# GNN kernel on one core: 64 source rows of every group are brought by SyncE's direct DMAs, and POOL's gathers of five chunks become shorter

## The chip, the core and the metric

One core of a Trainium2 chip. The number is the device time of one execution in microseconds (us), the median of several runs; lower is better.

## What is computed

Three layers of a relational graph network over 6250 nodes with 256 features, 200,000 edges sorted by destination, 8 edge types, and then a feed-forward layer on each node:

```python
for l in range(3):
    xr = jnp.einsum('nd,rde->rne', x, W_rel[l])
    msg = xr[edge_type, src]
    agg = jax.ops.segment_sum(msg, dst, num_segments=x.shape[0])
    x = jax.nn.relu(agg + x @ W_root[l] + bias[l])
# around it: x = x0 + gnn(layernorm(x0)); x = x + ffn(layernorm(x)), ffn in the log domain
```

The step that matters here is `msg[..., src]`: for every edge the 1 KB row of its source node is read from a table in HBM, 200,000 rows a layer.

## The kernel before, in words

The edges are cut into **chunks** of 128 (one edge a partition), three chunks make a **triple**, and nine triples (27 chunks, 3456 edges) a **group**. A layer has 58 groups, the last of which has 8 triples. Three layers make 174 groups.

The tile `rows` is a ring of 27 chunk slots, one group deep: slot (k, j) holds chunk j of triple k, 128 partitions by 256 floats.

- **POOL** (L393 to L403) fills the ring. For each chunk it issues one indirect DMA: 128 indices of `idx`, one row of the node table for each. Before triple k of a group it waits on `seg_ready` until TensorE has finished triple k of the group before, since it overwrites that slot. Each gather counts `gathered[k]` up by 16.
- **PE** waits for the three gathers of a triple (`rows_of`, L425), multiplies the rows by a one-hot matrix of (type, destination) (L421, 12 instructions a triple), and raises `seg_ready`. Once a group it multiplies the sums by the 8 relation matrices (L492).
- **DVE** adds the sums into `agg` (L1003), makes the one-hot matrices of the next group (L908) and adds a group's result to the node sums (L1025, L1026).
- **ACT** zeroes `agg`, and ends and stores finished tiles of 128 nodes.
- **SP** (SyncE) has little to do in layer 0: one 128 KB load of a node tile a group (`load_tile`, L329). In layers 1 and 2 it fetches the last chunk (8, 2) of every odd group but the last, row by row: it reads 32 source numbers into registers (L347), issues 32 one-row DMAs into the buffer `far_rows` (L352), and so four times. DVE copies `far_rows` into the ring slot at the head of the odd group (`take_fetched`, L969 to L975) and thereby frees the buffer for SP's next fetch. POOL leaves out that gather (the `CH - 1` of L398).

The order of POOL's gathers is the plain order of groups, triples and chunks. In the set-up SP issues the loads of the weights, of the source numbers for its own fetches (`far_idx`, L308) and of small tables, from which DVE makes the groups' places before the first product can start.

```python
for j in range(CH - 1 if layer and g % 2 and k == TPG - 1 else CH):
```

Of the kernel before, what the change touches and what calls it, by code (L numbers as in the profile page):

```python
# [7 lines left out]
P = 128  # L8
# [4 lines left out]
CH = 3  # L13
# [20 lines left out]
FETCHED = GROUPS // 2 - 1  # L34
HALF = P // 2
LOADS = 32
LN_EPS = 1e-5
LOG_EPS = 1e-8
assert TRIPLES == FULL_TRIPLES + 2 and 0 < TAIL < TE and BLOCKS == FULL_BLOCKS + 1 and TILES == XC * XCHUNKS + 1
assert WIN * R == P and GROUPS > TILES and GROUPS == 2 * FETCHED + 2  # L40


def gnn_ffn(nc, x, src, dst, etype, w_rel, w_root, gnn_bias, ffn_w, ffn_b, out):
    fp32, bf16 = mybir.dt.float32, mybir.dt.bfloat16
    i32, u32 = mybir.dt.int32, mybir.dt.uint32
# [7 lines left out]
    tables = [nc.dram_tensor(f"node_table{i}", [NP_, D], fp32, kind="Internal").ap() for i in range(2)]  # L53
    span_dram = nc.dram_tensor("triple_span", [2, BLOCKS * P], fp32, kind="Internal").ap()
# [5 lines left out]
    with ctx:  # L60
# [20 lines left out]

        far_idx = at("far_idx", [1, FETCHED * P], i32, edges_at)
        assert FETCHED * P * 4 <= 2 * edge_bytes
# [16 lines left out]
        far_rows = sb("far_rows", [P, D], fp32)  # L100
# [120 lines left out]
        far_idx_loaded = sem("far_idx_loaded")  # L221
        far_fetched = [[sem(f"far_fetched{l}_{h}") for h in range(2)] for l in range(1, L)]
        far_copied = sem("far_copied")
# [52 lines left out]
        def _(sp):  # L276
# [22 lines left out]
            for c, (lo, hi) in enumerate(x_chunks):  # L299
# [33 lines left out]
            with sp.Fori(0, TILES) as g:  # L333
                load_tile(g, g)
            with sp.Fori(TILES, GROUPS) as g:
                load_tile(g, TILES - 1)
            for layer in range(L - 1):
                sp.wait_ge(out_ready, (layer + 1) * GROUPS)
                sp.wait_ge(stored, 16 * TILES * (layer + 1) + 16)
                load_weights(layer + 1)  # L340
                sp.wait_ge(far_idx_loaded, 16)
                with sp.Fori(0, FETCHED) as i:

                    sp.wait_ge(far_copied, i * 2 + (layer * 2 * FETCHED + 2))
                    sp.sem_inc(sp_mark, 1)
                    for q in range(P // LOADS):
                        _, nodes = nc.values_load_multi_w_load_instructions(  # L347
                            far_idx[0:1, ds(i * P + q * LOADS, LOADS)], engines=[SP], min_val=0, max_val=N - 1,
                            skip_runtime_bounds_check_because="sources are nodes")
# [8 lines left out]
        def _(pool):  # L358
# [31 lines left out]
            for layer in range(L):  # L390
# [740 lines left out]
```

## Time and profile before

| what | us |
| --- | --- |
| median of 3 runs | 5964.4 |
| the runs | 5960.87 to 5973.35 |
| span of the profiled execution | 5964.9 |
| its own time beside the span | not given apart |
| POOL busy | 4396.5 (74%) |
| PE busy | 4310.7 (72%) |
| DVE busy | 1844.7 (31%) |
| ACT busy | 619.0 (10%) |

POOL's busy time is the time in which its cores work on a gather; what its sequencer needs between two gathers is not counted as busy, so 74% need not mean that POOL had time to spare. Issuing a DMA on SP is not counted as busy either and is read from the view of the line that issues it.

### The profile page before, as it was taken

What the parts mean: (1) busy time and instruction counts of PE and PEld (TensorE: products, weight loads), DVE (VectorE), ACT (ScalarE), POOL (GpSimd) and SP (SyncE); (2) the same over time, 40 slices, a digit from 0 to 9 for tenths busy, and PEclk for the clock granted to TensorE, in tenths of its full rate; (3) what the DMA queues carried; (4) which work ended last, traced back from release to release, by engine and by line L of the source; (5) the groups of instructions that cost most, each with busy time, mean ns of one, the idle gap of its engine ahead of it and who ended that gap; (6) DMA issues with size and microseconds to landing.
All of it is one profiled execution on the core that took longest, in us unless ns stands there. A gap on an engine that the chain in (4) does not pass through costs nothing.

```text
span 5964.9 us, 107654 instructions
## 1 busy us (share of the span) xinstructions
PE 4310.7 (72%) x26040; PEld 3901.4 (65%) x26041; DVE 1844.7 (31%) x3589; ACT 619.0 (10%) x848; POOL 4396.5 (74%) x4659
## 2 busy tenths in 40 slices
PE   4777777777777767777777777766776777776776
PEld 3666666666676656666666666666676666666666
DVE  5222222222222222222222222223333334333333
ACT  3001010010101000000000001000101011101111
POOL 5777777777777677777777777767777777777774
PEclk8898989898989888889999999888888888888887
DMA  6333333333333333333333333333333333333332
GB/s 196 113 111 113 112 112 112 111 114 111 113 112 112 107 111 110 111 111 111 110 111 111 111 110 112 110 106 113 114 113 115 113 113 114 114 113 114 113 113 74
DMA packets 296167, 674.77 MB, mean 113 GB/s; under 512 B 86202, under 2 KB 147387, under 8 KB 295772
## 3 DMA queue, kind: packets, MB, share of 16 engines
q0 software_dynamic: 222384, 607.55, 35.2%
q1 hardware_dynamic: 44686, 37.38, 2.1%
q10 hardware_dynamic: 28702, 26.46, 1.3%
q14 instruction: 378, 3.10, 0.2%
q8 instruction: 17, 0.28, 0.0%
HBM read 645.38 MB, written 25.68 MB: 112 GB/s over the span
## 4 chain that ended last, share of the span: by engine, by line
PE 27%; POOL 25%; issue 20%; SPq 15%; DMA 6%; DVEq 3%; DVE 3%; ACT 1%; ACTq 0%
POOL rows L403 25%; PE bank L421 15%; SPq L352 13%; PE bank L492 10%; DMA rows<-node_table,idx 5%; SPq L347 3%; DVE agg L1003 1%; ACT agg L708 1%; DVEq L986 1%; DVEq L989 1%; PE bank L618 1%; DVEq L1093 1%; PE bank L611 0%; DVE onehot L908 0%; PE bank L537 0%
## 5 line engine op out<-in xcount | busy, mean ns | idle before, releaser
L403 POOL DMA_INDIRECT rows<-node_table,idx x4633 | 4389.2, 947 | 1504.1 <-issue 1316.2
L421 PE MATMUL bank<-onehot,rows 128*128 128x128 f32 x18792 | 2700.1, 305 | 1422.5 <-DVE agg L1003 705.8
L421 PEld LDWEIGHTS bank<-onehot,rows 128*128 128x128 f32 x18792 | 2564.0, 218 | 1571.8 <-issue 1553.2
L1003 DVE TENSOR_TENSOR agg<-bank,agg 128x256 f32 x1566 | 663.7, 424 | 2079.8 <-PE bank L421 1575.6
L492 PE MATMUL bank<-wrel,agg 128*128 128x256 f32 x5568 | 1273.8, 388 | 44.4 <-DVE agg L1016 34.2
L492 PEld LDWEIGHTS bank<-wrel,agg 128*128 128x128 f32 x5568 | 1073.4, 195 | 200.0 <-issue 53.9
L908 DVE TENSOR_TENSOR onehot<-bank,key 128x1152 f32<-128x1152 f32 x525 | 707.0, 1347 | 0.0
L708 ACT COPY agg<-zero_col 128x2304 f32 x174 | 367.2, 2111 | 2928.9 <-PE bank L492 2928.9
L1025 DVE SCALAR_TENSOR_TENSOR acc<-bank,in_first,acc 128x256 f32 x174 | 84.2, 484 | 1777.6 <-PE bank L492 1680.9
L611 PE MATMUL bank<-wroot,nextT 128*128 128x256 f32 x392 | 146.7, 510 | 0.0
L715 ACT COPY acc<-bank 128x256 f32 (+1 forms) x98 | 36.5, 372 | 1004.7 <-PE bank L611 1004.7
L611 PEld LDWEIGHTS bank<-wroot,nextT 128*128 128x128 f32 x392 | 85.3, 241 | 55.2 <-issue 45.3
L599 PE MATMUL bank<-ident_bf,sgn 128*128 128x128 bf16 x98 | 16.2, 258 | 121.5 <-issue 115.1
L599 PEld LDWEIGHTS bank<-ident_bf,sgn 128*128 128x128 bf16 x98 | 6.5, 100 | 130.0 <-issue 130.0
L609 PE MATMUL bank<-bias_bc,one_row 1*128 1x256 f32 x196 | 90.3, 549 | 1.3 <-ACT nextT L723 1.3
L723 ACT COPY nextT<-bank 128x256 f32<-128x256 f32 x98 | 36.5, 372 | 462.2 <-PE bank L592 462.2
L1026 DVE SCALAR_TENSOR_TENSOR acc<-bank,in_second,acc 128x256 f32 x174 | 82.6, 475 | 0.0
L537 PE MATMUL bank<-wroot,xT 128*128 128x256 f32 x232 | 78.7, 474 | 0.0
L1016 DVE TENSOR_TENSOR agg<-agg 128x256 f32<-128x256 f32 (+1 forms) x174 | 72.7, 418 | 0.0
L537 PEld LDWEIGHTS bank<-wroot,xT 128*128 128x128 f32 x232 | 56.7, 248 | 11.0
L975 DVE COPY rows<-far_rows 128x256 f32<-128x256 f32 x56 | 19.1, 340 | 144.8 <-DMA far_rows<-node_table 113.6
L618 PE MATMUL bank<-wT,magT 128*128 128x256 f32 x196 | 51.4, 386 | 0.9 <-ACT sgnT L741 0.9
(138 smaller groups left out, 800.1 us busy)
## 6 DMA issues: line engine op xcount, KB each, us to landing
far_rows<-node_table SPq DMA_DIRECT2D x7168, 1.0 KB
rows<-node_table,idx POOLq DMA_INDIRECT x4633
node_table<-new_x ACTq DMA_DIRECT2D x98, 128.0 KB
x_tile<-node_table SPq DMA_DIRECT2D x58, 128.0 KB, 2.2
x_in<-in_x_dram SPq DMA_DIRECT2D x8, 768.0 KB, 11.2
wrel<-in_L_gnn_W_rel_dram SPq DMA_DIRECT2D x6, 1024.0 KB, 8.2
xres<-in_x_dram ACTq DMA_DIRECT2D x48, 128.0 KB
out_dram<-res ACTq DMA_DIRECT2D x48, 128.0 KB
```

The lines of the kernel that those rows point to most:

```text
L347: _, nodes = nc.values_load_multi_w_load_instructions(far_idx[0:1, ds(i * P + q * LOADS, LOADS)], engines=[SP], min_val=0, max_val=N - 1, ...
L352: sp.dma_start(far_rows[p:p + 1, :].rearrange("o (a b) -> o a b", a=2), tables[(layer + 1) % 2][ds(nodes[m], 1), :].rearrange("o (a b) -> ...
L403: pool.indirect_dma_start(rows[:, s:s + D], None, tables[layer % 2], bass.IndirectOffsetOnAxis(ap=idx[:, g * TPG + k, j:j + 1], axis=0),). ...
L421: last = nc.tensor.matmul(to[:, h, :], of[:, s:s + P], hot[:, hot_k * CH + j, :], start=(j == 0), stop=(j == CH - 1))
L492: last = nc.tensor.matmul(out_ps, agg[:, half * KH + h, r, 0:P], wrel[:, h, r * D:(r + 1) * D], start=(r == 0 and h == 0), stop=(r == R - ...
L537: last = nc.tensor.matmul(root_ps, xT[:, h, :], wroot[:, 0, h, :], start=(h == 0), stop=(h == KH - 1))
L609: nc.tensor.matmul(next_ps, one_row[:, :], bias_bc[0:1, layer + 1, :], start=True, stop=False)
L611: last = nc.tensor.matmul(next_ps, nextT[:, h, :], wroot[:, layer + 1, h, :], start=False, stop=(h == KH - 1))
L618: nc.tensor.matmul(lns_ps, magT[:, h, :], wT[:, h, :], start=(h == 0), stop=(h == KH - 1))
L708: nc.scalar.copy(agg[:, ds(g % 2 * KH, KH), :, :].rearrange("p h r s -> p (h r s)"), zero_col[:, :].to_broadcast([P, KH * R * SLOTS])).the ...
L908: return nc.vector.tensor_tensor(onehot[:, b, :, :], place_ps.unsqueeze(1).to_broadcast([P, BATCH * CH, P]), key[:, ds(g * TPG + b * BATCH ...
L1003: nc.vector.tensor_tensor(window, seg[k % 3].rearrange("p h (r w) -> p h r w", r=R), window, ALU.add).then_inc(agg_added, 1)
```

## The change

In all 57 full groups of all three layers, POOL's gathers of five chunks get shorter: chunks (7,1) and (7,2) by their last 4 rows, (8,0) by 8, (8,1) by 16, (8,2) by 32, 64 rows in all. SP brings these 64 rows by one-row DMAs straight into the ring slots. For that it waits, as POOL does, until triples 7 and 8 of the group before have been multiplied. The whole-chunk fetch, the buffer `far_rows`, DVE's copy and the left-out gather go away. SP's table of sources is now five strided loads from `src`, and DVE shifts it once so that it holds byte offsets; PE waits for SP's landings as well as for the gathers. The diff, cut to its core:

```diff
-FETCHED = GROUPS // 2 - 1
-HALF = P // 2
+FETCHED = GROUPS - 1
+TAILS = ((TPG - 2, 1, 4), (TPG - 2, CH - 1, 4), (TPG - 1, 0, 8), (TPG - 1, 1, 16), (TPG - 1, CH - 1, 32))
...
+    table_bytes = [t.rearrange("n d -> (n d)").bitcast(u8).unsqueeze(0) for t in tables]
...
             sp.wait_ge(turned, 11)
+            full_groups = src[0:FETCHED * TPG * TE].rearrange("(o g e) -> o g e", o=1, e=TPG * TE)
+            m = 0
+            for i, (k, j, n) in enumerate(TAILS):
+                end = (k * CH + j + 1) * P
+                q, m = (1, 0) if i == len(TAILS) - 1 else (0, m)
+                sp.dma_start(far_at[q:q + 1, :, m:m + n], full_groups[:, :, end - n:end]).then_inc(far_at_loaded, 16)
+                m += n
             load_weights(0)
-            full_groups = src[0:(GROUPS - 2) * TPG * TE].rearrange("(g e) -> g e", e=TPG * TE)
-            sp.dma_start(far_idx[:, :].rearrange("o (g e) -> o g e", e=P),
-                         full_groups[1::2, TPG * TE - P:TPG * TE].unsqueeze(0)).then_inc(far_idx_loaded, 16)
...
-            for layer in range(L - 1):
-                sp.wait_ge(out_ready, (layer + 1) * GROUPS)
-                sp.wait_ge(stored, 16 * TILES * (layer + 1) + 16)
-                load_weights(layer + 1)
-                sp.wait_ge(far_idx_loaded, 16)
-                with sp.Fori(0, FETCHED) as i:
-                    sp.wait_ge(far_copied, i * 2 + (layer * 2 * FETCHED + 2))
...
-                    for q in range(P // LOADS):
...
-                        for m in range(LOADS):
-                            p = q * LOADS + m
-                            sp.dma_start(far_rows[p:p + 1, :].rearrange("o (a b) -> o a b", a=2),
-                                         tables[(layer + 1) % 2][ds(nodes[m], 1), :].rearrange("o (a b) -> o a b", a=2)
-                                         ).then_inc(far_fetched[layer][p // HALF], 16)
+            def fetch(layer, g):
+                def tail(i, starts, landed):
+                    k, j, n = TAILS[i]
+                    s = (k * CH + j) * D
+                    for p, start in zip(range(P - n, P), starts):
+                        sp.dma_start(rows[p:p + 1, s:s + D].bitcast(u8), table_bytes[layer % 2][:, ds(start, ROW_BYTES)]).then_inc(landed, 16)
+
+                few = starts_of(g, 0, LOADS)
+                if layer or not isinstance(g, int):
+                    sp.wait_ge(seg_ready, g * TPG + (layer * TRIPLES - 1))
+                    sp.sem_inc(sp_mark, 1)
+                tail(0, few[0:4], far_in_eighth[layer])
+                tail(1, few[4:8], far_in_eighth[layer])
+                if layer or not isinstance(g, int):
+                    sp.wait_ge(seg_ready, g * TPG + layer * TRIPLES)
+                    sp.sem_inc(sp_mark, 1)
+                tail(2, few[8:16], far_in_ninth[layer][0])
+                tail(3, few[16:32], far_in_ninth[layer][0])
+                tail(4, starts_of(g, 1, LOADS), far_in_ninth[layer][1])
+
+            load_tile(0, 0)
+            sp.wait_ge(far_at_ready, 1)
+            fetch(0, 0)
+            load_tile(1, 1)
+            with sp.Fori(1, TILES - 1) as g:
+                fetch(0, g)
+                load_tile(g + 1, g + 1)
...
+            for layer in range(1, L):
+                sp.wait_ge(out_ready, layer * GROUPS)
+                load_weights(layer)
+                sp.wait_ge(stored, 16 * TILES * layer + 16)
+                with sp.Fori(0, FETCHED) as g:
+                    fetch(layer, g)
...
-                        for j in range(CH - 1 if layer and g % 2 and k == TPG - 1 else CH):
+                        for j in range(CH):
                             s = (k * CH + j) * D
+                            own = P - sum(n for *at, n in TAILS if at == [k, j] and g < FETCHED)
                             pool.indirect_dma_start(
-                                rows[:, s:s + D], None, tables[layer % 2],
-                                bass.IndirectOffsetOnAxis(ap=idx[:, g * TPG + k, j:j + 1], axis=0),
+                                rows[0:own, s:s + D], None, tables[layer % 2],
+                                bass.IndirectOffsetOnAxis(ap=idx[0:own, g * TPG + k, j:j + 1], axis=0),
                             ).then_inc(gathered[k], 16)
...
+                if k == TPG - 2:
+                    with pe.If(g < FETCHED):
+                        pe.wait_ge(far_in_eighth[layer], g * (16 * 8) + 16 * 8)
...
+                if k == TPG - 1:
+                    with pe.If(g < FETCHED):
+                        pe.wait_ge(gathered[k], g * (16 * CH) + (layer * FETCHED + 1) * (16 * CH))
+                        for h, n in ((0, 24), (1, LOADS)):
+                            pe.wait_ge(far_in_ninth[layer][h], g * (16 * n) + 16 * n)
...
+            dve.wait_ge(far_at_loaded, 16 * len(TAILS))
+            nc.vector.tensor_single_scalar(far_at[:, :, :], far_at[:, :, :], ROW_SHIFT, ALU.arith_shift_left).then_inc(far_at_ready, 1)
...
-            def take_fetched(layer, g):
...
-                nc.vector.tensor_copy(rows[:, s:s + D], far_rows[:, :]).then_inc(far_copied, 2)
```

POOL's instructions, before: the end of an odd group of layer 1 and the head of the next. Each row is one form of gather with how many follow one another; the second row is the last triple, with two gathers in place of three.

```order
L403 DMA rows<-node_table,idx 128x256 [waits seg_ready]
L403 DMA rows<-node_table,idx 128x256 x2
L403 DMA rows<-node_table,idx 128x256 [waits seg_ready]
L403 DMA rows<-node_table,idx 128x256
L403 DMA rows<-node_table,idx 128x256 [waits seg_ready]
L403 DMA rows<-node_table,idx 128x256 x2
```

POOL's instructions after the change, the last three triples of any full group and the head of the next:

```order
L432 DMA rows<-node_table,idx 128x256 [waits seg_ready]
L432 DMA rows<-node_table,idx 128x256 x2
L432 DMA rows<-node_table,idx 128x256 [waits seg_ready]
L432 DMA rows<-node_table,idx 124x256 x2
L432 DMA rows<-node_table,idx 120x256 [waits seg_ready]
L432 DMA rows<-node_table,idx 112x256
L432 DMA rows<-node_table,idx 96x256
L432 DMA rows<-node_table,idx 128x256 [waits seg_ready]
```

The number of gathers of an odd group goes from 26 to 27, and five of the 27 now cover fewer partitions.

SP's instructions, before: the head of the loop that fetches a chunk. The pair of rows at L352 stands 32 times behind each of the four loads of L347.

```order
L347 ISA [waits far_copied]
L347 TENSOR_LOAD far_idx
L352 ISA
L352 DMA far_rows<-node_table 1x256
L352 ISA
L352 DMA far_rows<-node_table 1x256
L352 ISA
```

SP's instructions after the change, one pass of the loop of layer 1 or 2 (in layer 0 a load of `x_tile` stands behind it):

```order
L341 TENSOR_LOAD far_at
L356 ISA
L352 DMA rows<-node_table 1x1024 [waits seg_ready]
L352 DMA rows<-node_table 1x1024 x7
L361 REGISTER_ALU
L352 DMA rows<-node_table 1x1024 [waits seg_ready]
L352 DMA rows<-node_table 1x1024 x23
L341 ISA
L341 TENSOR_LOAD far_at
L352 DMA rows<-node_table 1x1024 x32
```

One pass now serves one group in place of two, with 64 rows and two loads of registers; the address instruction ahead of each one-row DMA is gone, and the waits are on `seg_ready` and no longer on DVE's copy.

## Rows read from the trace of the kernel before

**Rows 1.** The page: span, busy time of each engine, and the gathers' group.

```profile
span 5964.9 us, 107654 instructions
...
PE 4310.7 (72%) x26040; PEld 3901.4 (65%) x26041; DVE 1844.7 (31%) x3589; ACT 619.0 (10%) x848; POOL 4396.5 (74%) x4659
...
L403 POOL DMA_INDIRECT rows<-node_table,idx x4633 | 4389.2, 947 | 1504.1 <-issue 1316.2
```

**Rows 2.** Timeline of POOL alone, layer 0, steady state: start, length, idle before.

```profile
1099.98 0.94 POOL L403 DMA_INDIRECT rows<-node_table,idx  x1 [0.30 <-PE bank L421]
1101.23 0.94 POOL L403 DMA_INDIRECT rows<-node_table,idx  x1 [0.30 <-issue]
1102.47 0.94 POOL L403 DMA_INDIRECT rows<-node_table,idx  x1 [0.30 <-issue]
1103.72 0.94 POOL L403 DMA_INDIRECT rows<-node_table,idx  x1 [0.30 <-issue]
```

**Rows 3.** The gathers by stretch: set-up, layers 0, 1, 2, the gaps, the end.

```profile
0.00:50.50 50.50, 0.00 (x0) 1.00 0.95 318
50.50:2011.30 1960.80, 1478.49 (x1563) 0.90 0.39 113
2011.30:2036.50 25.20, 0.00 (x0) 0.77 0.04 10
2036.50:3956.40 1919.90, 1452.18 (x1535) 0.90 0.39 112
3956.40:3982.60 26.20, 0.00 (x0) 0.70 0.03 11
3982.60:5908.90 1926.30, 1458.50 (x1535) 0.86 0.39 115
5908.90:5964.90 56.00, 0.00 (x0) 0.71 0.03 9
```

**Rows 4.** Line L403 over the whole span: shortest, median, longest gather, idle before.

```profile
L403 POOL DMA_INDIRECT rows<-node_table,idx x4633: 941/946/1201, 50.8 to 5907.8; - x194
```

**Rows 5.** Waits of POOL within 3000 to 3900 us (total, times, longest).

```profile
POOL rows L403 <- issue: 200.6, 658, 0.3
POOL rows L403 <- PE bank L421: 18.9, 62, 0.3
```

**Rows 6.** SP's lines in the window 2118.6 to 2184.8 us, one fetch of 128 rows.

```profile
L352 SPq FUSED_REGOPS  x128: 37/37/37, 2120.8 to 2183.4; - x128
L352 SPq MOVE far_rows<-node_table x128: 29/29/29, 2120.9 to 2183.5; - x128
L352 SPq DMA_DIRECT2D far_rows<-node_table x128: 224/225/282, 2120.9 to 2183.6; - x128
...
L347 SPq TENSOR_LOAD <-far_idx x5: 2028/2030/2032, 2118.7 to 2183.9; - x5
```

**Rows 7.** Timeline of SP, 32 one-row DMAs between two register loads.

```profile
2120.92 13.26 SPq L352 DMA_DIRECT2D far_rows<-node_table  x32
```

**Rows 8.** DMA queue of the gathers (packets, MB, share of 16 engines).

```profile
q0 software_dynamic: 222384, 607.55, 35.2%
```

**Rows 9.** Chain that ended last, 3000 to 3200 us: the landing of a gather.

```profile
3027.14 2.72 DMA rows<-node_table,idx
```

**Rows 10.** Timeline of SP in the set-up.

```profile
50.63 1.01 SPq L279 DMA_DIRECT2D wrel<-in_L_gnn_W_rel_dram  x2
51.68 1.60 SPq L308 DMA_DIRECT2D far_idx<-in_src_dram  x1
53.33 1.55 SPq L311 DMA_DIRECT2D wroot<-in_L_gnn_W_root_dram  x3
54.92 1.88 SPq L314 DMA_DIRECT2D span<-triple_span  x2
```

**Rows 11.** Timeline of POOL, the first gather of the second group.

```profile
90.94 0.94 POOL L403 DMA_INDIRECT rows<-node_table,idx  x1 [6.40 <-PE bank L421]
```

**Rows 12.** DVE's copy of a fetched chunk, over the whole span.

```profile
L975 DVE COPY rows<-far_rows x56: 281/294/543, 2101.1 to 5846.5; 128x256 f32<-128x256 f32 x56
```

More of the change, by code:

```diff
@@ L32 @@
 XCHUNKS = 8
[L34 to L35 removed]
+FETCHED = GROUPS - 1
+TAILS = ((TPG - 2, 1, 4), (TPG - 2, CH - 1, 4), (TPG - 1, 0, 8), (TPG - 1, 1, 16), (TPG - 1, CH - 1, 32))
 LOADS = 32
+ROW_BYTES = D * 4
+ROW_SHIFT = 10
 LN_EPS = 1e-5
@@ L39 @@
 assert TRIPLES == FULL_TRIPLES + 2 and 0 < TAIL < TE and BLOCKS == FULL_BLOCKS + 1 and TILES == XC * XCHUNKS + 1
-assert WIN * R == P and GROUPS > TILES and GROUPS == 2 * FETCHED + 2
+assert WIN * R == P and GROUPS > TILES and ROW_BYTES == 1 << ROW_SHIFT
 def gnn_ffn(nc, x, src, dst, etype, w_rel, w_root, gnn_bias, ffn_w, ffn_b, out):
     fp32, bf16 = mybir.dt.float32, mybir.dt.bfloat16
-    i32, u32 = mybir.dt.int32, mybir.dt.uint32
+    i32, u32, u8 = mybir.dt.int32, mybir.dt.uint32, mybir.dt.uint8
     ALU = mybir.AluOpType
@@ L219, in gnn_ffn @@
         w_taken = sem("w_taken")
-        far_idx_loaded = sem("far_idx_loaded")
-        far_fetched = [[sem(f"far_fetched{l}_{h}") for h in range(2)] for l in range(1, L)]
-        far_copied = sem("far_copied")
+        far_at_loaded = sem("far_at_loaded")
+        far_at_ready = sem("far_at_ready")
+        far_in_eighth = [sem(f"far_in_eighth{l}") for l in range(L)]
+        far_in_ninth = [[sem(f"far_in_ninth{l}_{h}") for h in range(2)] for l in range(L)]
         gathered = [sem(f"gathered{k}") for k in range(TPG)]
@@ new lines, in starts_of @@
+            def starts_of(g, q, n):
+                _, starts = nc.values_load_multi_w_load_instructions(
+                    far_at[q:q + 1, ds(g, 1), 0:n].rearrange("q g m -> q (g m)"), engines=[SP], min_val=0, max_val=(N - 1) * ROW_BYTES,
+                    skip_runtime_bounds_check_because="sources are nodes")
+                return starts
+            def fetch(layer, g):
[7 more added lines that the diff above has]
+                    sp.wait_ge(seg_ready, g * TPG + (layer * TRIPLES - 1))
+                    sp.sem_inc(sp_mark, 1)
+                tail(0, few[0:4], far_in_eighth[layer])
[6 more added lines that the diff above has]
+                tail(4, starts_of(g, 1, LOADS), far_in_ninth[layer][1])
@@ new lines, in _ @@
+            load_tile(0, 0)
[5 more added lines that the diff above has]
+                load_tile(g + 1, g + 1)
+            with sp.Fori(TILES - 1, FETCHED) as g:
+                fetch(0, g)
+                load_tile(g + 1, TILES - 1)
+            for layer in range(1, L):
[4 more added lines that the diff above has]
+                    fetch(layer, g)
@@ L428, in rows_of @@
                     pe.wait_ge(gathered[k], gg * (16 * CH) + 16 * CH)
-                elif layer == 0:
-                    with pe.If(g < GROUPS - 1):
-                        pe.wait_ge(gathered[k], g * (16 * CH) + 16 * CH)
+                if k == TPG - 2:
+                    with pe.If(g < FETCHED):
+                        pe.wait_ge(far_in_eighth[layer], g * (16 * 8) + 16 * 8)
                         pe.sem_inc(pe_mark, 1)
-                else:
-                    before = (GROUPS - 1) * 16 * CH + (layer - 1) * 16 * ((GROUPS - 1) * CH - FETCHED)
-                    with pe.If(g < GROUPS - 1):
-                        with pe.If(g % 2 > 0):
-                            pe.wait_ge(gathered[k], g * (16 * CH - 8) + (before + 16 * CH - 8))
-                            pe.wait_ge(far_copied, g + ((layer - 1) * 2 * FETCHED + 3))
-                            pe.sem_inc(pe_mark, 1)
-                        with pe.Else():
-                            pe.wait_ge(gathered[k], g * (16 * CH - 8) + (before + 16 * CH))
-                            pe.sem_inc(pe_mark, 1)
+                if k == TPG - 1:
[3 more added lines that the diff above has]
+                            pe.wait_ge(far_in_ninth[layer][h], g * (16 * n) + 16 * n)
                         pe.sem_inc(pe_mark, 1)
@@ L967, in extra_tiles @@
                     dve.sem_inc(dve_mark, 1)
-            def take_fetched(layer, g):
-                for h in range(2):
-                    dve.wait_ge(far_fetched[layer - 1][h], g * (8 * HALF) + 8 * HALF)
-                held(g)
-                s = (TPG * CH - 1) * D
-                nc.vector.tensor_copy(rows[:, s:s + D], far_rows[:, :]).then_inc(far_copied, 2)
             def group(layer, g, late=None):
                 gg = g + layer * GROUPS
-                if layer == 1 and g % 2 and g < GROUPS - 1:
-                    take_fetched(layer, g)
-                if layer == L - 1:
-                    with dve.If(g < GROUPS - 1):
-                        with dve.If(g % 2 > 0):
-                            take_fetched(layer, g)
-                        dve.sem_inc(dve_mark, 1)
                 _, places = nc.values_load_multi_w_load_instructions(
```

13 lines of the change are left out of this document (2 added, 11 removed).

## The prediction, made before the changed kernel was run

> **What bounds the kernel now.** I read the page first, then POOL alone in time, then the gathers by stretch, then SP. On the page no engine is busy over 74%, and POOL and PE stand level [rows 1]. The timeline decides between them: POOL's gathers start every 1.25 us, 0.94 to 0.95 us of work and 0.30 us between, without a break [rows 2]. The view of the line says that this holds throughout: 4633 gathers, the median 946 ns, the shortest 941 [rows 4]. By stretch the three layers are nothing but this beat: layer 0 has 1563 gathers in 1960.8 us, layer 1 has 1535 in 1919.9, layer 2 has 1535 in 1926.3, that is 1.254, 1.251 and 1.255 us each [rows 3]. What stands as a wait for PE in front of a gather is never longer than the 0.3 us which also stands where POOL waits for nothing [rows 5], so the ring never holds POOL up. The rest of the span is 50.5 us of set-up, two gaps of 25 and 26 us between layers and 56 us at the end. **So the time is the number of gathers times POOL's 1.251 us, plus about 158 us.** PE has room: it follows POOL, and idle time of PE costs nothing as long as it does.
>
> The only cover that matters is thus POOL's. Page and trace give the profiled execution as a span of 5964.9 us, no other time apart; the median of the runs is 5964.4, so both agree within 0.5 us and I add the sum to the median.
>
> **The change part by part.**
>
> *Gathers that come back.* Layers 1 and 2 left out one gather in each of 28 odd groups, 56 in all (DVE's 56 copies count them [rows 12]). Each is again a gather: 56 x 1.251 = +70.1 us, all on POOL's path. This is the one large term that is sure, whatever the rows cost.
>
> *Rows that leave POOL.* In 3 x 57 = 171 groups, five gathers shrink by 64 rows in all; 171 x 64 = 10,944 rows. The trace has no gather of fewer than 128 rows, so the price of a row on POOL must be bounded. From below: nothing, if a gather costs what it costs by the instruction. From above: the whole 946 ns divided by 128, 7.4 ns a row, which gives 0.473 us a group and 10,944 x 7.4 ns = 80.9 us. The 0.30 us between two gathers I leave out of that, since it is there before any gather has begun; with it the bound would be 9.8 ns and 107 us. Nor is the other sign excluded: the longest gather of 128 rows took 1201 ns [rows 4], and five such in each group would add 5 x 0.255 x 171 = 218 us; but shorter instructions of the same kind have no reason that I see to be longer, and this end gets little chance. Between 0 and 7.4 no row is nearer than another. I take the middle, 3.7 ns: the 946 ns must hold a part for starting and for telling the 16 engines, and a part for the addresses. That gives -40.5 us.
>
> *A rule on this price.* In the trace a gather of 128 rows and 131 KB takes 946 ns of POOL whatever stands beside it [rows 4], and no row separates rows from start. The Trainium skill (DMA: Bandwidth & Descriptors, Anatomy of one DMA) calls descriptor generation "small, variable" and says that many descriptors can be emitted before their cost is seen; by that rule the saving is nothing and the sum is 6037 us, which is the first rival.
>
> *SP's work.* In a fetch, SP issues 32 rows in 13.26 us, 0.41 us a row, of which 37 + 29 + 225 ns are its three instructions and 0.12 us the gaps between them; the address instruction of 37 ns falls away with its gap of some 0.04. A register load takes 2.03 us [rows 6, 7]. At 0.34 us a row a group costs 64 x 0.34 + 2 x 2.1 = 26 us; at the old 0.41 it would be 30.6 us. The group lasts 27 x 1.25 = 33.8 us less the saving. So SP has 3 to 7 us to spare, and its cost is nothing, with that cover. The chain within a group is also short enough: from the end of triple 8 of one group SP issues 24 rows (8.2 us), loads registers (2.1), issues 32 rows (10.9) and the last lands some 2 to 3 us later (a gather lands in 2.7 [rows 9]): 24 us. PE needs them when POOL's last gather lands, a beat of 33.5 us later. In front of x_tile's load in layer 0 now stands the fetch; PE transposes in the middle of the next group, and the load is issued some 26 us into this one, so it is in time.
>
> *Added waits.* PE waits at triples 7 and 8 for SP's landings; behind it stand triple 8's products, and POOL waits for these only when it comes to the same slots a group later. PE may be late by tens of microseconds before POOL feels it. The first group is the tightest: SP starts on it at about 85 us, and is done at about 112 with 64 rows, while POOL wants slot 8 free at about 91 + 24 x 1.25 = 121. Nothing.
>
> *DVE.* 56 copies of 294 ns go [rows 12], one small shift comes, both off the path. Nothing.
>
> *Set-up.* One load of 1.60 us [rows 10] is replaced by five strided ones ahead of the weights. Two strided loads of 58 pieces took 1.88 us there [rows 10], so five take 4.7 us: 3.1 us more before `span` is loaded, from which DVE makes what PE starts with. POOL's second group waited 6.4 us for PE's first product [rows 11], so this delay passes on in full: +3 us (1 to 6).
>
> Sum: 5964.4 + 70.1 - 40.5 + 3 = **5997 us**, 0.5% slower.
>
> **The rivals.**
>
> *A gather costs by the instruction.* For it: the beat is so even. Against it: the 946 ns must do something for 128 separate addresses. Time: 5964.4 + 70.1 + 3 = 6037.5 us.
>
> *A gather costs by the row.* The five save 80.9 us: 5964.4 + 70.1 - 80.9 + 3 = 5957 us, no change that can be told. It needs a start of nothing within the 946 ns; the 0.30 us of gap may be all the start there is.
>
> *A gather costs by the engines it is dealt to* (the other side, faster). The gathers' queue has 222,384 packets for 4633 gathers, exactly 48 each, three for each of 16 engines [rows 8]. If 124 rows (not a multiple of 16) go out on fewer engines, a share of POOL's work that is done once per engine falls away. If all 946 ns were of that kind, 59 ns an engine, and both gathers of 124 rows went to 4 engines, a group would save 2 x 12 x 59 ns = 1.42 us and the one of 120 rows on 15 engines another 0.06: 253 us. With half of it, 127 us and no saving by rows: 5964.4 + 70.1 - 127 + 3 = 5911 us. The change turns faster where a group saves more than 0.43 us. For it: something must be done for each engine. Against it: nothing in the trace shows an uneven gather. The Trainium skill (DMA: Bandwidth & Descriptors, Why a DMA increments its semaphore by 16 and not by 1) says that a DMA takes the largest number of engines up to 16 that divides its partitions, which would be 4 for 124 and 15 for 120; it says nothing of the price on POOL. The transfers could bear it: 35.2% of 16 engines for 593,024 rows is 57 ns a row [rows 8], so 31 rows on one engine take 1.8 us in place of 0.5.
>
> *SP becomes the bound* (slower). It decides from 0.45 us a row, (33.3 - 4.2) / 64. At 0.50 us a group would take 36.2 us, and 171 groups 500 us more: 6500. The measured 0.41 with a longer instruction list speaks against it.
>
> **How the numbers follow.** A measurement of this kernel can tell 0.2%, 12 us. Chances: my forecast's mixture (1 to 5 ns a row, 5982 to 6030) 0.31; by the instruction 0.25; by the row 0.14; faster through engines, or through the gap's share, 0.27; SP or longer partial gathers 0.03. The first two and the last are slower, 0.58 with a little of the third taken off; the third is the same, 0.15; faster 0.27. The range runs from 5905, just below the half-way price of the engines' case, to 6042, above the dearest of the fixed price with the set-up's upper end. Left out are the deeper half of the engines' case and SP's, some 0.15. The likeliest case alone spans 5982 to 6030.
>
> **What the profile after would show.** The gathers' line must have 4689 instructions (4633 + 56). Apart by rows, the shapes of 124, 120, 112 and 96 would tell the price: 946 ns for all by the instruction, 710 ns for 96 by the row, about 830 by my middle, and a gather of 124 far shorter than one of 112 by the engines. The packets of the gathers' queue tell the engines: 48 for each gather if all 16 still take part. SP's one-row DMAs must number 10,944, 0.34 us apart; a wait of POOL for PE longer than 0.3 us in mid-layer would say that SP's rows hold up the ring, and then everything above about POOL's price is beside the point. The first gather of the second group should start at about 94 us. I am wrong if the beat of the full gathers, 1.25 us, changes.

## The result, and the profile after

The changed kernel took 6163.9 us, the median of 4 runs (6159.31 to 6165.94), against 5968.9 (5960.87 to 5975.14) for the kernel before, measured beside it: 1.0326 of before, 95% interval 1.0312 to 1.0341. It is 195 us slower. The forecast was 5997 with a range up to 6042, so the direction was right and the size was not. On one of the chips used (the slow chip below), the kernel before took 8394 to 8489 us; six of the kernels below were first run there, and from those runs only the lengths of single gathers are used (a full one took 0.946 us there too).

The page after, answering to [rows 1] and [rows 8]; the numbers of the gathers' group are busy time, mean length and idle time before:

```profile
span 6163.1 us, 108925 instructions
...
PE 4438.8 (72%) x26040; PEld 4013.3 (65%) x26041; DVE 1827.1 (30%) x3534; ACT 618.9 (10%) x848; POOL 4580.1 (74%) x4715
...
q0 software_dynamic: 257904, 604.20, 34.6%
...
L432 POOL DMA_INDIRECT rows<-node_table,idx x4689 | 4572.8, 975 | 1533.6 <-issue 1362.5
```

There are 56 gathers more, as counted, but POOL's busy time rose by 184 us, and the mean gather became longer, 975 ns in place of 947, though five in each group fetch fewer rows. POOL alone in time, from the last full gathers of a group on, shows which ones:

```profile
3012.87 0.94 POOL L432 DMA_INDIRECT rows<-node_table,idx  x1 [0.30 <-PE bank L450]
3014.11 1.29 POOL L432 DMA_INDIRECT rows<-node_table,idx  x1 [0.30 <-issue]
3015.71 1.29 POOL L432 DMA_INDIRECT rows<-node_table,idx  x1 [0.30 <-issue]
3017.31 0.98 POOL L432 DMA_INDIRECT rows<-node_table,idx  x1 [0.30 <-issue]
3018.60 0.95 POOL L432 DMA_INDIRECT rows<-node_table,idx  x1 [0.30 <-issue]
3019.86 0.92 POOL L432 DMA_INDIRECT rows<-node_table,idx  x1 [0.30 <-issue]
3021.08 0.96 POOL L432 DMA_INDIRECT rows<-node_table,idx  x1 [0.30 <-issue]
3022.34 0.95 POOL L432 DMA_INDIRECT rows<-node_table,idx  x1 [0.30 <-issue]
```

In order of the program these are: a full gather, then 124, 124, 120, 112 and 96 rows, then two full ones of the next group. The two gathers that leave out only 4 rows take 1.29 us, 0.35 more than a full one. The one of 96 rows saves 0.03. The gaps are 0.30 as ever, and no gather waits for SP. Over the groups the medians are 1.292, 1.295, 0.985, 0.954 and 0.915 us, and 0.963 and 0.951 for the next two full ones, where 0.946 is usual: together +0.73 us a group, in 171 groups 125 us.

The gathers by stretch, answering to [rows 3]:

```profile
0.00:51.00 51.00, 0.00 (x0) 1.00 0.95 314
51.00:2060.00 2009.00, 1521.99 (x1563) 0.88 0.39 111
2060.00:2089.00 29.00, 0.00 (x0) 0.77 0.27 82
2089.00:4086.40 1997.40, 1521.07 (x1563) 0.85 0.37 106
4086.40:4116.40 30.00, 0.00 (x0) 0.72 0.25 81
4116.40:6122.40 2006.00, 1529.70 (x1563) 0.87 0.38 109
6122.40:6163.10 40.70, 0.00 (x0) 0.68 0.03 10
```

Against before: layer 0 +48.2 us, layers 1 and 2 +77.5 and +79.7 (35 each of that are the 28 gathers which came back), the two gaps +7.6, the end of the kernel -15.3, set-up +0.5, in all +198.2, the difference of the spans. The end is shorter since PE no longer stands far behind POOL when the last gather is out. Its products of the last group's sums (L492 before, L515 now) start 29 us behind the end of the last gather before (5908.9) and 14 us behind it now (6122.2):

```profile
5937.97 9.43 PE L492 MATMUL bank<-wrel,agg 128*128 128x256 f32 x32 [4.19 <-issue]
```

```profile
6136.17 9.42 PE L515 MATMUL bank<-wrel,agg 128*128 128x256 f32 x32 [4.20 <-issue]
```

SP's work is as light as was said. In the first group it issued 64 rows, with one load of registers (2.1 us) among them, in 23.3 us, 0.33 us a row. Over the whole span SP waits for PE at the slot of triple 7 (L357) 165 times, 1185 us in all, so it is ahead of the ring:

```profile
91.74 23.34 SPq L352 DMA_DIRECT2D rows<-node_table  x64
```

```profile
SPq L357 <- PE bank L450: 1185.3, 165, 11.0
```

### The profile page after: what moved, and what is told of

Read it like the earlier page. It is cut to its first block, busy times and chain, and to the rows that moved or that the text cites. A ratio compares the mean times of both kernels' runs of the same rounds, so it can differ in the third digit from the quotient of the medians.

```text
span 6163.1 us, 108925 instructions
## 1 busy us (share of the span) xinstructions
PE 4438.8 (72%) x26040; PEld 4013.3 (65%) x26041; DVE 1827.1 (30%) x3534; ACT 618.9 (10%) x848; POOL 4580.1 (74%) x4715
## 4 chain that ended last, share of the span: by engine, by line
POOL 42%; PE 27%; issue 18%; DMA 8%; ACT 2%; DVEq 2%; DVE 1%; SPq 0%; ACTq 0%; POOLq 0%
POOL rows L432 42%; PE bank L450 15%; PE bank L515 8%; DMA rows<-node_table,idx 7%; PE bank L634 2%; ACT agg L731 1%; PE bank L632 1%; DVE agg L1013 1%; PE bank L560 1%; DVEq L996 0%; DVEq L999 0%; DVEq L1103 0%; ACT x_in L687 0%; DMA node_table<-new_x 0%; PE bank L641 0%
## 5 line engine op out<-in xcount | busy, mean ns | idle before, releaser
L432 POOL DMA_INDIRECT rows<-node_table,idx x4689 | 4572.8, 975 | 1533.6 <-issue 1362.5
L450 PE MATMUL bank<-onehot,rows 128*128 128x128 f32 x18792 | 2773.9, 311 | 1548.7 <-DMA rows<-node_table,idx 860.7
L450 PEld LDWEIGHTS bank<-onehot,rows 128*128 128x128 f32 x18792 | 2643.3, 223 | 1689.2 <-issue 1663.5
L515 PE MATMUL bank<-wrel,agg 128*128 128x256 f32 x5568 | 1273.6, 388 | 10.7 <-issue 9.0
L515 PEld LDWEIGHTS bank<-wrel,agg 128*128 128x128 f32 x5568 | 1073.2, 195 | 164.3 <-issue 16.1
L634 PE MATMUL bank<-wroot,nextT 128*128 128x256 f32 x392 | 180.7, 608 | 0.0
L634 PEld LDWEIGHTS bank<-wroot,nextT 128*128 128x128 f32 x392 | 103.2, 291 | 71.4 <-issue 56.8
L632 PE MATMUL bank<-bias_bc,one_row 1*128 1x256 f32 x196 | 110.3, 660 | 1.3 <-ACT nextT L746 1.3
L560 PE MATMUL bank<-wroot,xT 128*128 128x256 f32 x232 | 95.6, 558 | 0.0
L560 PEld LDWEIGHTS bank<-wroot,xT 128*128 128x128 f32 x232 | 67.7, 296 | 15.3
L632 PEld LDWEIGHTS bank<-bias_bc,one_row 1*128 1x128 f32 x196 | 46.8, 296 | 23.5 <-issue 23.3
```

Of the source, the lines that this page charges most:

```text
L432: pool.indirect_dma_start(rows[0:own, s:s + D], None, tables[layer % 2], bass.IndirectOffsetOnAxis(ap=idx[0:own, g * TPG + k, j:j + 1], ax ...
L450: last = nc.tensor.matmul(to[:, h, :], of[:, s:s + P], hot[:, hot_k * CH + j, :], start=(j == 0), stop=(j == CH - 1))
L515: last = nc.tensor.matmul(out_ps, agg[:, half * KH + h, r, 0:P], wrel[:, h, r * D:(r + 1) * D], start=(r == 0 and h == 0), stop=(r == R - ...
L560: last = nc.tensor.matmul(root_ps, xT[:, h, :], wroot[:, 0, h, :], start=(h == 0), stop=(h == KH - 1))
L632: nc.tensor.matmul(next_ps, one_row[:, :], bias_bc[0:1, layer + 1, :], start=True, stop=False)
L634: last = nc.tensor.matmul(next_ps, nextT[:, h, :], wroot[:, layer + 1, h, :], start=False, stop=(h == KH - 1))
```

## The experiments

Three theories of the long gathers were open. **Padding**: rows are dealt evenly to the largest number of DMA engines, up to 16, that divides their count; an engine that gets none is given as many small filler entries as the others get rows, and POOL writes them all. **Contention**: SP's one-row DMAs, in flight beside POOL, slow it. **Flat penalty**: any uneven gather costs some 0.35 us more. The packets after already speak for padding. Before, each gather made 48 packets [rows 8]. Now 3834 full gathers make 184,032, and the rest, 73,872, is 432 for each of 171 groups. A full gather is 32 packets of 4096 bytes, four rows in each, and 16 packets of 4 bytes for the semaphore. By padding a gather of 124 rows goes to 4 engines, 31 rows each, which are 8 packets, and to 12 engines with 8 packets of filler each, with 16 packets of semaphores 144 in all; those of 120, 112 and 96 rows make 48 each: 2 x 144 + 3 x 48 = 432. The sizes agree too: the trace after has 170 packets of 16 bytes and 24 of 12 a group, none of which occur before, and 31 filler entries of 4 bytes are seven packets of 16 bytes and one of 12 (2 gathers x 12 engines x 7, and 2 for the idle engine of the 120 rows, make 170; 2 x 12 make 24).

**Prices of gathers, even.** In a kernel where SP fetches nothing, row counts per chunk:

```diff
+SIZES = (128, 112, 128, 96, 128, 80, 128, 64, 128, 48, 128, 32, 128, 16, 128, 8, 128, 120, 128, 104, 128, 128, 124, 124, 120, 112, 96)
...
+                            own = SIZES[k * CH + j] if (layer or g) and g < GROUPS - 1 else P
...
-                                rows[:, s:s + D], None, tables[layer % 2],
+                                rows[0:own, s:s + D], None, tables[layer % 2],
...
```

> POOL alone gathers, SP brings no rows, and between full gathers stand single ones of 112, 96, 80, 64, 48, 32, 16, 8, 120 and 104 rows; at the group's end stand 124, 124, 120, 112 and 96 as in the change. The rows left out are not brought at all, so the sums of this kernel lack them. Padding theory: POOL writes 16 x (rows per engine) descriptors, at about 1 ns each above a fixed 820 ns, where the rows are dealt to the largest number of engines up to 16 that divides them. Then: 112 rows 930 ns, 96 rows 915, 64 rows 884, 32 rows 853, 16 rows 837, 8 rows (8 engines) 837, 120 and 104 about 946, and 124 still about 1292, with no row of SP's in flight. Contention theory (SP's one-row DMAs slow POOL while they run): 124, 120, 112 and 96 all at 946 or below, none above. By-the-row theory (the bound of 7.4 ns a row): 64 rows 473 ns, 16 rows 118 ns.

Timeline of POOL in this kernel, the chunks of 128, 112, 128, 96, 128 and 80 rows of one group, and then, further on, 128, 124, 124:

```profile
3268.20 0.96 POOL L392 DMA_INDIRECT rows<-node_table,idx  x1 [0.30 <-issue]
3269.47 0.93 POOL L392 DMA_INDIRECT rows<-node_table,idx  x1 [0.31 <-issue]
3270.70 0.97 POOL L392 DMA_INDIRECT rows<-node_table,idx  x1 [0.30 <-issue]
3271.97 0.91 POOL L392 DMA_INDIRECT rows<-node_table,idx  x1 [0.30 <-issue]
3273.19 0.96 POOL L392 DMA_INDIRECT rows<-node_table,idx  x1 [0.30 <-issue]
3274.45 0.90 POOL L392 DMA_INDIRECT rows<-node_table,idx  x1 [0.30 <-issue]
...
3300.28 0.95 POOL L392 DMA_INDIRECT rows<-node_table,idx  x1 [0.30 <-issue]
3301.54 1.30 POOL L392 DMA_INDIRECT rows<-node_table,idx  x1 [0.31 <-issue]
3303.15 1.30 POOL L392 DMA_INDIRECT rows<-node_table,idx  x1 [0.30 <-issue]
```

Medians over the groups: 128 rows 0.967 us, 112 0.927, 96 0.914, 80 0.901, 64 0.902, 48 0.872, 32 0.866, 16 0.852; 8 rows 0.881 (8 engines idle; 0.837 had been expected), 120 and 104 0.983 and 0.987. **A row is worth about 1 ns on POOL** ((967 - 852) / 112), and seven eighths of the gather are paid for 16 rows as well. The 124 are at 1.30 with SP idle, so contention falls as their cause. What I had not expected: a full gather next to a shorter one takes 0.967 and not 0.946, so a single short gather first pays 0.02 us to its neighbour; the runs give no cause for it. The page of this kernel gives 244,112 packets for the gathers' queue; the padding rule, worked out for all 27 sizes, gives 244,112.

**Prices of gathers, uneven.** The same with 126, 125, 121, 118, 110, 100, 88, 72, 62, 60, 60, 4 and 4 rows between full gathers.

> As before, POOL alone, with single gathers of 126, 125, 121, 118, 110, 100, 88, 72, 62, 60, 60, 4, 4 rows between full ones; the rows left out are not brought. Padding theory (820 ns + 0.95 ns x 16 x rows per engine): 126 on 14 engines, 9 each, 957 ns; 125 on 5, 25 each, 1200; 121 on 11, 11 each, 987; 118 on 2, 59 each, 1717; 110 on 11, 10 each, 972; 100 on 10, 10 each, 972; 88 on 11, 8 each, 942; 72 on 12, 6 each, 911; 62 on 2, 31 each, 1291, the same as 124 with half the rows; 60 on 15, 4 each, 881; 4 on 4, 1 each, 835. Flat-penalty theory (whatever is not dealt to all 16 engines pays some 350 ns once): 126, 125, 121, 118, 110, 100, 88, 72, 62 and 60 all between 1.2 and 1.3 us. By rows alone: lengths fall from 126 to 4 in order, 62 at about 880.

Timeline of POOL, the chunks of 128, 126, 128, 125, 128, 121, 128, 118 rows, and further on of 128, 62, 128, 60:

```profile
3278.16 0.95 POOL L392 DMA_INDIRECT rows<-node_table,idx  x1 [0.30 <-issue]
3279.41 0.99 POOL L392 DMA_INDIRECT rows<-node_table,idx  x1 [0.30 <-issue]
3280.71 0.97 POOL L392 DMA_INDIRECT rows<-node_table,idx  x1 [0.30 <-issue]
3281.99 1.20 POOL L392 DMA_INDIRECT rows<-node_table,idx  x1 [0.30 <-issue]
3283.49 0.97 POOL L392 DMA_INDIRECT rows<-node_table,idx  x1 [0.30 <-issue]
3284.77 1.01 POOL L392 DMA_INDIRECT rows<-node_table,idx  x1 [0.30 <-issue]
3288.33 0.98 POOL L392 DMA_INDIRECT rows<-node_table,idx  x1 [2.55 <-remote]
3289.61 1.65 POOL L392 DMA_INDIRECT rows<-node_table,idx  x1 [0.30 <-issue]
...
3303.14 0.97 POOL L392 DMA_INDIRECT rows<-node_table,idx  x1 [0.30 <-issue]
3304.42 1.28 POOL L392 DMA_INDIRECT rows<-node_table,idx  x1 [0.31 <-issue]
3306.01 0.96 POOL L392 DMA_INDIRECT rows<-node_table,idx  x1 [0.30 <-issue]
3307.27 0.92 POOL L392 DMA_INDIRECT rows<-node_table,idx  x1 [0.30 <-issue]
```

A gather of 62 rows costs 1.277 us, close to the 1.30 of one of 124, and both are dealt 31 to an engine; 60 rows, two fewer, cost 0.916. (The 2.55 us `remote` in front of one gather is idle time of the slow chip, where this kernel ran; it is not part of a gather's length.) Entries, rows and filler together, are 16 times the rows per engine, and the length follows them:

| rows | engines x rows | entries | median us | 0.902 + 0.806 ns x (entries - 16) |
| --- | --- | --- | --- | --- |
| 4 | 4 x 1 | 16 | 0.902 | fitted |
| 126 | 14 x 9 | 144 | 0.990 | 1.005 |
| 121 | 11 x 11 | 176 | 1.012 | 1.031 |
| 125 | 5 x 25 | 400 | 1.203 | 1.212 |
| 62 | 2 x 31 | 496 | 1.277 | 1.289 |
| 118 | 2 x 59 | 944 | 1.650 | fitted |

A flat penalty is out (100 rows, on 10 engines, take 0.998), and so is a price by rows. The queue's packets are again those of the padding rule, 290,352 on the page and by the count. The four rows between the fitted ends lie within 20 ns of the line, and the other uneven counts (110, 100, 88, 72 and 60 rows: 0.996, 0.998, 0.972, 0.943 and 0.916) within 25 ns below it. The line is fitted afterwards; the formula on record, 820 ns + 0.95 ns an entry, was 67 ns too low at 4 rows and 67 ns too high at 118, and the even counts lie about 50 ns under the new line (16 rows: 0.852 against 0.902).

One thing these runs can't tell apart: entries are always 16 times the rows per engine, so "POOL writes every filler entry" and "POOL's time goes with the longest share of one engine" give the same lengths. That the filler exists is seen in the packets; that it is what POOL spends the time on is the likelier reading and is not shown.

**No fetch at all.** POOL gathers everything, 4689 full gathers, SP idle; SP's loop and the waits for it are gone too.

```diff
-                        for j in range(CH - 1 if layer and g % 2 and k == TPG - 1 else CH):
+                        for j in range(CH):
```

> POOL gathers every row, 4689 gathers of 128, SP fetches none; the whole computation is there. Both theories of the price of a row agree: before's time plus 56 x 1.251 = 70 us, less what SP's late fetches cost at the end of the last layer (PE ended 29 us behind POOL's last gather before, 14 us after the change), so 6024 to 6039 us. It is the kernel against which each way of bringing rows by SP is to be read. If SP's fetches in the kernel before had cost POOL nothing and gained 70, this comes out 1.0% slower than before.

The first run, on the slow chip, gave 7360 against 8489 for the kernel before (0.868, 0.866 to 0.869) and says nothing of the terms. A row of the product's line (L408) shows what differs: the idle time of PE and of its weight loads, taken together, that nothing in the profile released. First in that run, then in the second run:

```profile
  issue: 2883.4, 1869
```

```profile
  issue: 1656.6, 836
```

> POOL gathers every row and SP fetches none, the whole computation. Run once more since in the first run PE and POOL stood still for long stretches in the middle of instructions that wait for nothing, in every kernel of that call, the kernel before too. Where they don't: 5969 + 70 (56 gathers of 1.251 us) less up to 15 at the end of the last layer, so 6024 to 6039 us, or 1.009 to 1.012 of before.

Measured: 6020.0 us against 5970.2, 1.0084 (1.0067 to 1.0101), +50 us. The 56 gathers are 70, and the end of the kernel, from the last gather on, is 41.1 us in place of 56.1: 70 - 15 = 55; 6024 to 6039 had been expected. So the whole-chunk fetch of the kernel before had gained 50 us, and not 70. That SP's late fetches had left PE behind in the last layer is borne out further down: with the same whole chunks, but 47.5 us from a fetch's first row to its last in place of 59.5, the end is 43.6 us and not 56.1.

**Even tails.** The change with 64 rows as 16, 16 and 32 of the chunks of triple 8.

```diff
-TAILS = ((TPG - 2, 1, 4), (TPG - 2, CH - 1, 4), (TPG - 1, 0, 8), (TPG - 1, 1, 16), (TPG - 1, CH - 1, 32))
+TAILS = ((TPG - 1, 0, 16), (TPG - 1, 1, 16), (TPG - 1, CH - 1, 32))
```

> The change with its 64 rows taken as the last 16, 16 and 32 of the three chunks of triple 8, so that 112, 112 and 96 rows are left, all dealt to 16 engines; triple 7 is gathered whole. Padding theory: the two gathers of 124 rows cost 0.346 us more each than full ones and the one of 120 about 0.04, 0.73 us a group in 171 groups, 125 us; without them 6164 - 125 - 5 = 6034 us. Contention theory: the same 64 rows run beside POOL at the same time, so it stays within 10 us of 6164. Flat price of partial gathers (any gather under 128 rows): 3 in place of 5 partial ones, 6164 x less two fifths of the excess, 6110.

The first run, on the slow chip, gave 7622 us (0.898 of its before, 0.8965 to 0.8995), for its gathers of 112, 112 and 96 rows 0.930, 0.935 and 0.912 us, and 0.967 for the next.

> The change with 16, 16 and 32 rows taken from the three chunks of triple 8 alone, whole computation; once more for the same reason. From the price of each gather in the first run (112 rows 0.930 and 0.935, 96 rows 0.912, the first full one behind them 0.967, others 0.949 us) a group costs 27 x 1.251 - 0.016 - 0.011 - 0.034 + 0.021 + 22 x 0.003 = 33.80 us against 33.78 without SP: the 64 rows buy nothing. Padding theory: 6024 to 6045 us, within 10 us of the kernel without any fetch, and 120 to 140 us below the change. Rival (SP's one-row DMAs hold POOL or PE up): near 6164.

Measured: 6020.6 us, 1.0083 (1.0067 to 1.0100). That is the kernel without any fetch (6020.0) to within a microsecond, and 143 us below the change; 6024 to 6045 had been expected. POOL in this kernel, a full gather, then 112, 112, 96, then the next full ones:

```profile
3014.09 0.95 POOL L427 DMA_INDIRECT rows<-node_table,idx  x1 [0.30 <-issue]
3015.34 0.93 POOL L427 DMA_INDIRECT rows<-node_table,idx  x1 [0.30 <-PE bank L445]
3016.58 0.93 POOL L427 DMA_INDIRECT rows<-node_table,idx  x1 [0.30 <-issue]
3017.81 0.91 POOL L427 DMA_INDIRECT rows<-node_table,idx  x1 [0.30 <-issue]
3019.03 0.97 POOL L427 DMA_INDIRECT rows<-node_table,idx  x1 [0.30 <-PE bank L445]
```

This separates the two parts of the loss: 50 us for giving up the whole-chunk fetch, and 143 us for the 4- and 8-row tails, of which POOL's gathers themselves explain 137 (4572.8 us busy in the change, 4436.0 here). The 10,944 rows that SP brings cost and gain nothing that the time shows. In the two profiles POOL's gathers are 6 us shorter in all with SP's rows (4436.0 against 4442.1; 0.07 us saved a group, 0.02 given to the neighbour), and the second gap between the layers is 4 us longer (30.2 against 25.9).

**The change's gathers without SP's rows.** Row counts as in the change, SP idle, the rows left out are missing from the sums.

```diff
+SIZES = (128, 128, 128, 128, 128, 128, 128, 128, 128, 128, 128, 128, 128, 128, 128, 128, 128, 128, 128, 128, 128, 128, 124, 124, 120, 112, 96)
...
```

> POOL's gathers exactly as in the change (124, 124, 120, 112, 96 at the end of each full group but the first of layer 0), and SP brings none of the rows: the sums lack them. Padding theory: two gathers of 1.30 us in place of 0.946, +0.73 us a group, so the kernel without any fetch (6020) + 170 x 0.73 = 6144 us, 15 to 20 under the change at most. Contention theory: with SP idle the gathers are 0.95 or less and it stays at 6020. If both have a part, between.

First run, on the slow chip: 7241.5 us, 0.863 (0.861 to 0.864) of a before that took 8393.7; not usable for the terms.

> Once more where all engines run as in the profile of before: POOL's gathers as in the change, SP brings none of the rows. Padding theory: 6020 + 170 x 0.73 = 6144 us (1.029 of before). Contention theory: 6020 (1.008). What is left up to the change's 6164 is SP's.

Measured: 6151.9 us, 1.0301 (1.0283 to 1.0318), +132 over the kernel without fetch, of which 170 x 0.73 = 124 were expected. In its profile every full gather is 3 ns longer than in the others (0.949 us), 14 us in all, which covers the rest. By the medians SP's rows and the new table own 12 of the change's 195 us; since the four runs of this kernel lie 19 us apart (6146.5 to 6165.9), those 12 are uncertain by some 10 either way. The 124 rows take 1.295 and 1.298 us with SP idle, so contention is ruled out as the main cause a second time.

**Late table.** The five strided loads behind the loads of the spans.

```diff
+            full_groups = src[0:FETCHED * TPG * TE].rearrange("(o g e) -> o g e", o=1, e=TPG * TE)
...
             sp.wait_ge(meta_ready, 1)
```

> The change with its five strided table loads behind the loads of the spans and not ahead of the weights. In the change the second group's first gather began at 97.2 us, 6.3 later than before. If the five loads' place in SP's queue is the cause, it begins at 91 to 92 and the whole is 5 to 6 us below 6164; if it is SP's 64 rows of the first group or the added DVE step, it stays at 97.

One run: 6159.9 us, 4 below the median of the change and within the range of its runs. The second group's first gather, in the change and in this kernel:

```profile
97.23 0.96 POOL L432 DMA_INDIRECT rows<-node_table,idx  x1 [11.03 <-PE bank L450]
```

```profile
93.60 0.96 POOL L432 DMA_INDIRECT rows<-node_table,idx  x1 [7.65 <-PE bank L450]
```

It begins 3.6 us earlier, not 5 to 6. But in the kernel without fetch, whose loads stand as in before, this gather began at 94.2 and not at 90.9. So one profile against another differs by 3 us here with the loads in the same place, and the 3.6 us can't be told from that.

**Whole chunks in all layers.** What a left-out gather saves is its 1.251 us; rows save nothing. So fetching whole chunks, as before, is the better form, and layer 0 lacked it. It uses the change's byte offsets, with which SP issues a row every 0.32 us in place of 0.41.

```diff
+                        for j in range(CH - 1 if g % 2 and g < GROUPS - 1 and k == TPG - 1 else CH):
...
+            def half(layer, i, h):
+                for q in range(h * 2, h * 2 + 2):
+                    _, starts = nc.values_load_multi_w_load_instructions(
+                        far_idx[0:1, ds(i * P + q * LOADS, LOADS)], engines=[SP], min_val=0, max_val=(N - 1) * ROW_BYTES,
...
+                        sp.dma_start(far_rows[p:p + 1, :].bitcast(u8), table_bytes[layer % 2][:, ds(starts[m], ROW_BYTES)]
+                                     ).then_inc(far_fetched[layer][h], 16)
...
+            with sp.Fori(1, HALVES) as i:
+                fetch(0, i, i * 2)
+                load_tile(i * 2 + 1, i * 2 + 1)
```

> The kernel before with its whole-chunk fetch in layer 0 as well, and with the byte-offset table and the one-row DMA of the change; no partial gather anywhere. A left-out gather saves 1.251 us whatever the price of rows: 28 more of them are -35 us, the earlier end of SP's fetches (52 us for 128 rows in place of 62) -15 at the end, a stall while the first fetch lands (SP starts at 83 us, needs 52) up to +10: 5925 us, 0.993 of before. Rival (SP, which also loads a node tile each group, becomes the bound in layer 0): groups of layer 0 longer than 33.8 us a pair's half, above 5969.

Measured: 5935.2 us against 5970.2, 0.9941 (0.9924 to 0.9957), 10 above what was expected. The rival's long groups are not there: the two groups of a pair in layer 0 take 33.8 and 32.5 us. A wait of 7 us stands where it was expected. The row names PE as the releaser; PE waits for DVE there, and DVE, which copies at the group's head, waits 21.1 us for the first fetch:

```profile
145.00 0.94 POOL L426 DMA_INDIRECT rows<-node_table,idx  x1 [7.08 <-PE bank L444]
```

**The copy in mid group.** DVE's copy moved from the head of the odd group behind the sixth triple.

```diff
+                    if k == TPG - 4:
+                        take(layer, g)
```

> The kernel with whole chunks by SP in all layers (5935 us), but DVE copies the fetched chunk into the ring behind the sixth triple's sums in place of the group's head. There, POOL's third group waited 7 us for the first fetch. If DVE's early copy is that wait, it is gone: 5935 - 7 = 5928 us. If the copy in mid group makes PE late at the last triple, each pair of groups gains up to 1 us, up to 5970. The fallback for groups spread over many tiles, which these inputs never take, is given up in it.

First run, on the slow chip: 7530.2 us, 0.897 (0.895 to 0.898) of a before at 8393.7.

> Once more for the same reason: whole chunks by SP in all layers, copied in mid group. 5928 us if the head-of-group copy was the 7 us wait at the start; up to 5970 if the later copy holds up PE.

Measured: **5922.6 us, 0.9923 (0.9907 to 0.9940)**, the fastest here: its runs (5921.7 to 5930.3) all lie below those with the copy at the head (5932.5 to 5937.0), though the intervals of the two ratios overlap. The 7 us wait is gone, and POOL's beat is untouched: layer 0 now takes 1928.3 us for its 1535 gathers.

```profile
50.90:1979.20 1928.30, 1454.65 (x1535) 0.92 0.40 115
```

## Why the prediction was right and wrong

- **The bound.** Right. Before and after, the time is POOL's sequence of gathers with 0.30 us between. In the eight profiles at the usual speed no gap within a layer is over 0.32 us but those at the second group of layer 0 (6.2 to 11.0 us) and the 7.1 us of the first whole-chunk fetch in layer 0.
- **Gathers that come back, +70.1 us.** Right: 4689 gathers, and layers 1 and 2 are each 35 us longer for it. This term is what made the direction right. Missing beside it was the 15 us at the end, which the fetch of before had cost and which the change gives back; I had read the 56 us behind the last gather as a constant.
- **Rows that leave POOL, -40.5 us.** This is the step that failed, in size and in sign: the assumption that a gather of fewer rows is shorter. I took the middle of 0 to 7.4 ns a row. It is 1 ns where the count is a multiple of 16, some 0.05 us a group with the neighbour's share, and the kernel without fetch and the one with even tails differ by 0.6 us. With the tails of the change it is +125 us, against -40.5. "The middle, since no row is nearer" was no reason: the first rival had the better one, the even beat. The Trainium skill's sentence in DMA: Bandwidth & Descriptors, Anatomy of one DMA, that many descriptors can be emitted before their cost is seen, agrees with the 1 ns a row, and does not cover the filler.
- **The far end that I gave little chance.** I bounded longer partial gathers by the longest gather seen, +218 us, and dismissed it because "shorter instructions of the same kind have no reason that I see to be longer". They have one, the uneven dealing, which stood in the third rival.
- **A gather costs by the engines it is dealt to.** The dealing was right: 124 rows on 4 engines, 120 on 15, which is what the Trainium skill states (DMA: Bandwidth & Descriptors, Why a DMA increments its semaphore by 16 and not by 1), and the packets agree to the last one. The price had the wrong sign. I let the idle engines save 59 ns each; the packets show that each of the 12 is given 31 entries of filler, and the gather is 0.35 us longer.
- **SP hidden.** Right, and right in size: 0.33 us a row, some 26 us a group. The even tails show it as time: 0.6 us, which is nothing.
- **Added waits, DVE.** Nothing, as said. PE waited 8.35 us for SP's rows in the first group, and POOL's gaps behind it stay at 0.30.
- **Set-up, +3 us (1 to 6).** In its range, but not shown: the second group's first gather begins 6.3 us later than before (97.2 against 90.9), 3.6 us earlier again with the late table, and 3 us of such a difference come and go with the loads unmoved.
- **The gaps between layers** were taken as unchanged and came out at 29.0 and 30.0 us, 4 us longer each. Two things in the views by stretch go with it. The change issues the next layer's weights before it waits for the layer's last stores, so that the DMA share in the gaps is 0.27 and 0.25 in place of 0.04 and 0.03, and the granted clock of TensorE in the gap differs from profile to profile. Of the ten gaps with the weights in them (in five kernels), four at a granted clock of 0.86 to 0.92 are 24.7 to 26.3 us long and six at 0.67 to 0.82 are 27.3 to 30.1. The six gaps without them, at 0.70 to 0.82, are 25.0 to 26.7. No run changes one of the two alone, so the cause stays open, at 8 us of 195.

With the measured prices, and 4 us for the set-up, the sum is 5968.9 + 70 + 125 - 15 + 4 + 8 = 6161 us, 3 below what was measured. Most of these terms are read from the change's own profile, so their sum is a check that nothing large is missing; what tests the cause is that 124 us come back with the uneven gathers alone (132 measured) and 143 go away with even ones.

## What to carry to other kernels

Where POOL's gathers bound a kernel, count instructions, not rows: 16 rows cost 0.85 us and 128 rows 0.95, so what pays is to leave whole gathers out. If a gather must be shortened, keep its count a multiple of 16; a count whose largest divisor up to 16 is small (124, 62, 118) costs up to 0.7 us more than the full 128, and even 126, 121, 120, 110 and 100 rows cost 0.04 to 0.07 more. And when a mechanism can share out work unevenly, ask for its price with both signs before giving one end of the range no weight.

## What the runs showed of the hardware

An indirect gather's length on POOL is about 0.9 us plus 0.8 ns for each of 16 x (rows per engine) entries when it is uneven, 1 ns a row when it is even. An engine without rows gets filler packets, 4 bytes for each row that a working engine gets: 170 packets of 16 bytes and 24 of 12 a group in the change, none before. A full gather beside a shorter one is 0.02 to 0.03 us longer (0.963 behind the group's end in the change, 0.967 and 0.977 between short ones, against 0.946).

On one chip the same kernel before took 8.4 to 8.5 ms in place of 5.97, at a mean granted clock of 0.76 in place of 0.88. In the kernel without fetch full gathers (0.946 us) and the median product of L408 (275 ns) had the same length there, and PE had more idle time that nothing released. The kernels that let SP fetch lost more on it than those in which SP is idle: 7360 us with no fetch and 7622 with even tails, beside 8489 before; 7241 with the change's gathers and no fetch and 7530 with whole chunks in mid group, beside 8394 before. These runs give no cause for it.
